# Routing the Gelu experts of a four-stage transformer kernel, and spreading the spline weights' preparation

## What is computed

```python
# layer 0: neighbourhood attention; layer 2: window attention with a bias and a mask
# layer 1: Gelu experts, 2 shared and 8 routed, each token takes its best 2
hs = gelu(einsum('td,nfd->ntf', t, sw1) + sb1); shared = einsum('ntf,ndf->td', hs, sw2) + sb2.sum(0)
probs = softmax(t @ gate_w.T + gate_b); top_v, top_i = top_k(probs, 2)
routed = sum over the two chosen e of top_v * (gelu(t @ rw1[e].T + rb1[e]) @ rw2[e].T + rb2[e])
# layer 3: spline experts, 8, each token takes its best 2
spline = einsum('nic,oic->no', b_splines(x), spline_w * scaler[..., None])
```

## Time and profile before

| | us |
|---|---|
| median of 3 runs | 1057.26 |
| lowest, highest | 1048.71, 1076.12 |
| span of the profiled execution | 1046.9 |
| busy: PE, DVE, ACT, POOL | 937.1, 663.3, 632.8, 377.1 |

### The profile page before, as it was taken

How to read it: one execution, slowest core, us unless ns; L and a number is a source line. 1 busy time by engine, 2 the same in 40 slices (tenths; PEclk the granted TensorE clock), 3 DMA queues, 4 the chain that set the end, 5 groups by cost and what they waited for, 6 DMA issues and landing times. The chain is left out here.

```text
span 1046.9 us, 23408 instructions
## 1 busy us (share of the span) xinstructions
PE 937.1 (90%) x8217; PEld 864.7 (83%) x8217; DVE 663.3 (63%) x1339; ACT 632.8 (60%) x1665; POOL 377.1 (36%) x298
## 2 busy tenths in 40 slices
PE   4776888999998886888979999999999999999993
PEld 3655777889987775766449999999999999999992
DVE  4766675452566534555854877877777777777762
ACT  5993433334442434996135788777777777777751
POOL 1225693882956911331011123223333323332111
PEclk9995898999999987675979999999999999999997
DMA  2002736458447330001134554531535442530000
GB/s 74 3 2 67 301 157 275 183 200 366 192 173 332 136 136 13 3 2 45 44 111 179 190 200 139 196 116 34 192 100 193 134 161 95 193 100 13 7 7 8
DMA packets 25100, 132.67 MB, mean 127 GB/s; under 512 B 3258, under 2 KB 14788, under 8 KB 17876
## 3 DMA queue, kind: packets, MB, share of 16 engines
q0 software_dynamic: 11152, 65.54, 17.5%
q1 hardware_dynamic: 13892, 66.39, 17.3%
HBM read 98.83 MB, written 33.10 MB: 126 GB/s over the span
## 5 line engine op out<-in xcount | busy, mean ns | idle before, releaser
L1242 PE MATMUL kan_ps_h<-kan_xf,kan_w 128*128 128x128 f32 x2496 | 304.4, 275 | 2.0 <-DMA kan_w<-w_dram 2.0
L1242 PEld LDWEIGHTS kan_ps_h<-kan_xf,kan_w 128*128 128x128 f32 x2496 | 291.2, 192 | 2.8 <-DMA kan_w<-w_dram 2.8
L675 ACT ACTIVATE f_hid<-f_ps_up,f_wt 128x512 f32<-128x512 f32 x160 | 108.4, 688 | 154.6 <-PE f_ps_up L624 154.4
L1256 PE MATMUL kan_ps_y<-kan_w,kan_hf 128*128 128x128 f32 x1248 | 154.0, 277 | 8.3 <-DVE kan_hf L1394 8.3
L635 PEld LDWEIGHTS f_ps_dn<-f_wt,f_hid 128*128 128x128 f32 x1280 | 149.7, 194 | 6.9 <-issue 3.1
L1256 PEld LDWEIGHTS kan_ps_y<-kan_w,kan_hf 128*128 128x128 f32 x1248 | 147.2, 194 | 8.8 <-issue 8.8
L635 PE MATMUL f_ps_dn<-f_wt,f_hid 128*128 128x128 f32 x1280 | 150.2, 277 | 3.4 <-DVE x_sb L745 3.4
L624 PE MATMUL f_ps_up<-f_n_part,f_w_part 128*128 128x512 f32 x480 | 127.3, 419 | 23.5 <-DVE f_w_part L704 17.4
L1465 POOL DMA_INDIRECT out<-kan_y_sb,kan_slots_y x39 | 63.8, 1636 | 234.5 <-ACT kan_y_sb L1340 234.5
L745 DVE SCALAR_TENSOR_TENSOR x_sb<-f_ps_dn,f_mix_now,x_sb 128x128 f32<-128x128 f32 x160 | 44.6, 343 | 137.6 <-PE f_ps_dn L635 137.4
L624 PEld LDWEIGHTS f_ps_up<-f_n_part,f_w_part 128*128 128x128 f32 x480 | 94.1, 202 | 43.7 <-DVE f_w_part L704 14.8
(11 more groups left out here) (197 smaller groups left out, 1572.7 us busy)
## 6 DMA issues: line engine op xcount, KB each, us to landing
kan_w<-w_dram SPq DMA_DIRECT2D x16, 2304.0 KB, 9.0
sw_raw<-in_experts POOLq DMA_DIRECT2D x8, 3456.0 KB, 15.4
w_dram<-sw_raw POOLq DMA_DIRECT2D x8, 2304.0 KB, 7.3
kan_w<-w_dram SPq DMA_DIRECT2D x16, 1152.0 KB, 5.2
w_dram<-sw_raw POOLq DMA_DIRECT2D x8, 1152.0 KB, 10.1
f_wt<-in_experts SPq DMA_DIRECT2D x10, 514.0 KB, 4.5
sw_scal<-in_scalers POOLq DMA_DIRECT2D x8, 384.0 KB, 16.4
x_sb<-in_x SPq DMA_DIRECT2D x4, 256.0 KB, 3.9
```

Source lines behind the costliest of these rows:

```text
L675: eng.activation(hid[s % 2][:, c, :], ps_up[c][:, :], ACT.Gelu, bias=wt[a][:, 2 * FF0 + c:2 * FF0 + c + 1]).then_inc(acted.sem, 1)
L1242: mm = eng.matmul(ps_h[n % 2][:, m, :], w12[n % 2][:, at:at + P], rhs, start=(c == 0), stop=(c == BASES))
L1256: mm = eng.matmul(ps_y[n % 2][:, :], lhs, w3[n % 2][:, i * P:(i + 1) * P], start=(i == 0), stop=(i == CH1 * FEAT - 1))
```

## The change

1. The Gelu layer runs only the two shared experts over all tiles (8 steps, with two `ps_up` buffers). For the eight routed ones VectorE forms the list of slots beside these steps, as the routing stage does. Then 39 tiles follow: GpSimd gathers 128 token rows from a DRAM copy of the normalised tokens, PE turns them, multiplies up and down in f32, VectorE scales, GpSimd scatters the rows to a DRAM array with two rows per token. SP loads the tile's expert (514 KB and a bias row), four buffers deep. At the end SP loads the two rows per token back and VectorE adds them.
2. The spline weights are prepared in 18 pieces of 128x512 per expert (`SplineWeights.piece`). Experts 0 to 2 are done by GpSimd in attention 0, three pieces a turn from turn 2; 3 and 4 by VectorE among the 39 tiles, two pieces a tile in tiles 0 to 8 and 30 to 38; 5 to 7 by GpSimd in attention 1 from turn 3. SP issues all their loads and stores. The window biases are added by VectorE in tiles 13 to 27.

```diff
@@ attention, GpSimd's loop
                     normalise(i - 5)
+                    beside(eng, i)
@@ build, attention 0 (attention 1: experts 5 to 7, i - 3 and i - 2)
+                def load0(eng):
...
+                    prep.load(eng, 0)
+                    prep.load(eng, 1)
+                    prep.store(eng, 0)
+                    prep.load(eng, 2, 0)
+                    prep.store(eng, 1)
+                    prep.store(eng, 2)
+                    for e in range(3):
+                        eng.wait_ge(prep.stored[e], 32)
...
+                def beside0(eng, i):
+                    for j in range(3 * (i - 2), 3 * (i - 1)):
+                        if 0 <= j < 3 * prep.PIECES:
+                            prep.piece(eng, j // prep.PIECES, j % prep.PIECES)
@@ SplineWeights
+    def store(self, eng, e):
+        eng.wait_ge(self.done[e], self.PIECES)
...
+    def piece(self, eng, e, j):
...
+        if j == 0:
+            eng.wait_ge(self.loaded[e], 32)
+        if j < BASES:
+            eng.tensor_tensor(first[:, j, :], first[:, j, :], scal[:, 0:SCAL12], ALU.mult).then_inc(self.done[e], 1)
...
@@ gelu_experts, SP
+                for n in range(SLOT_TILES):
+                    if n >= W_BUFFERS:
+                        eng.wait_ge(r_down, n - W_BUFFERS + 1)
+                    lot = eng.value_load(lots[0:1, n:n + 1], min_val=SHARED, max_val=SHARED + EXPERTS - 1)
+                    eng.dma_start(wt[n % W_BUFFERS][:, :], d["experts0"][bass.ds(lot, 1), :, :])\
+                       .then_inc(in_w[n % W_BUFFERS], 16)
...
+                    if n == 14:
+                        prep.store(eng, 3)
+                    if n == 22:
+                        prep.load(eng, 4, 3)
@@ gelu_experts, PE: turn_x waits for the gathered rows, tile_down for ScalarE's Gelu
+                turn_x(0)
+                turn_x(1)
+                tile_up(0)
+                for n in range(SLOT_TILES):
+                    turn_x(n + 2)
+                    tile_up(n + 1)
+                    tile_down(n)
@@ gelu_experts, GpSimd (X_BUFFERS is 4)
+                for n in range(X_BUFFERS):
+                    gather_x(n)
+                eng.wait_ge(slots_ok, 1)
+                for n in range(SLOT_TILES):
+                    scatter_y(n)
+                    gather_x(n + X_BUFFERS)
```

More of the change, by code:

```diff
@@ L487, in rank_experts, with gelu_experts @@
     first = earlier.rearrange("p (a b) -> p a b", b=EXPERTS).unsqueeze(1).to_broadcast(shape)
[L488 to L496, removed]
+    eng.tensor_tensor(above, other, own, ALU.is_gt)
+    chain.after(eng.tensor_tensor(level, other, own, ALU.is_equal))
+    chain.after(eng.tensor_tensor(level, level, first, ALU.mult))
+    chain.after(eng.tensor_tensor(above, above, level, ALU.add))
+    chain.after(eng.tensor_reduce(rank[:, :, :], above, X, ALU.add))
+def gelu_experts(nc, sems, clear_after, software, x_sb, consts, d, prep, make_bias, to_clear, stats, normed_dram, y_dram,
+                 pos1, mask1, s_tab):
     ident = consts[:, C_ID:C_ID + P]
+    ones = consts[:, C_ONES:C_ONES + P]
     with ExitStack() as own:
@@ new lines, in gelu_experts @@
+        picked = sb("picked", wide)
+        base = sb("base", wide)
+        total = sb("total", wide)
+        upto = [sb(f"upto{i}", wide) for i in range(2)]
+        many = sb("many", [P, EXPERTS, TILES])
+        tiles_of = sb("tiles_of", [P, EXPERTS])
+        before = sb("before", [P, EXPERTS, EXPERTS])
+        start = sb("start", [P, EXPERTS])
+        begun = sb("begun", [P, SLOT_TILES, EXPERTS])
+        owner = sb("owner", [P, SLOT_TILES])
+        lots = sb("lots", [P, SLOT_TILES], U32)
@@ L597, in _ @@
                 mm.then_inc(gated, 1)
[L598 to L615, removed]
@@ new lines, in _ @@
+                eng.wait_ge(counted, 1)
+                chain.after(eng.tensor_copy(total[:, :, :], ps_total))
+                chain.after(eng.tensor_copy(upto[0][:, :, :], total[:, :, :]))
+                a, step = 0, 1
+                while step < TILES:
+                    new, old = upto[1 - a], upto[a]
+                    eng.tensor_copy(new[:, 0:step, :], old[:, 0:step, :])
+                    chain.after(eng.tensor_tensor(new[:, step:, :], old[:, step:, :], old[:, 0:TILES - step, :],
+                                                  ALU.add))
+                    a, step = 1 - a, 2 * step
@@ new lines, in _ @@
+                chain.after(eng.tensor_reduce(start[:, :], before[:, :, :], X, ALU.add))
+                chain.after(eng.tensor_scalar(start[:, :], start[:, :], float(P), None, ALU.mult))
+                shape = [P, SLOT_TILES, EXPERTS]
+                chain.after(eng.tensor_tensor(begun[:, :, :], start[:, :].unsqueeze(1).to_broadcast(shape),
+                                              starts.unsqueeze(2).to_broadcast(shape), ALU.is_le))
+                chain.after(eng.tensor_reduce(owner[:, :], begun[:, :, :], X, ALU.add))
```

739 lines of the change are left out of this document (481 added, 258 removed).

## The result

The changed kernel takes 1091.8 us (median; 1086.91 to 1100.78). The kernel before has a median of 1066.69 in the same comparison, but two of its four runs (1076 and 1085 us) were slow ones, and the ratio, 1.0406 with a 95% interval of [1.0286, 1.0525], is taken from fast runs alone. The change is slower, as forecast; the forecast of 1078 was 14 us short. The profiled execution has a span of 1085.1 us, 38.2 longer than before's 1046.9 (forecast: 1073).

The account below looks back on a forecast made before the run. PE was taken to bound the Gelu layer, with GpSimd becoming the bound of attention 0. Attention 0 +27, attention 1 +33 and Gelu layer -34 gave +26 us on a span of 1046.9: 1073, plus 5 for 1078 us, range 1025 to 1122.

Parts of the forecast that it names:

- Attention 0, +27 forecast: Attention 0: first piece at about 20 us, GpSimd's 54 pieces, then the last store; stage ends near 116.5, +27 us.
- the loss of 0.3 at each normalisation: Attentions: GpSimd and VectorE's normalisation take turns, GpSimd losing some 0.3 us a time, 4.8 us for the stage.
- Attention 1, +33 forecast: Attention 1: the same 54 pieces, multiplications and additions between load and last store; 120 us against 87.5, +33.
- the store of expert 4 takes 6 us of the stage before the load: Attention 1: expert 4's store reaches 6 us into the stage, weights land at 7, the first expert's load at 17.
- Gelu layer, -34 forecast: Gelu layer: first y at 89 us, tiles 167, store and load 7, tail 17; 280 against 313.9, -34.
- The mechanism of the tile loop: Gelu layer's 39 tiles: gather n+4 stands behind scatter n on GpSimd; 8.8 us for two turns, 4.4 a tile.
- the way from y to GpSimd's scatter: Tile loop: y on VectorE, 0.28 us for a 128x128 and two semaphores, 0.6 us of the 8.8 for two tiles.
- need less: Tile loop: the tile weights, 514 KB a tile in four buffers, have three turns and need less than the chain.
- The spline store and load: Tile loop: expert 3's store and expert 4's load share the tile weights' queue and delay some tiles, +7 us.
- The loop at its floor: Rival, 0.20: tile loop at 3.25 us a tile, not 4.4; sum -22 us, 1030; decides from 3.7 a tile down.
- The blocked normalisation: Rival, 0.17: VectorE's normalisation enters only when GpSimd stops; +36 us in attention 0, +4 in attention 1, 1118 us.
- The half clock: Rival, 0.18: PE at half clock through the tile loop, with the longer scatter; 5.15 us a tile, +29, 1107 us.

Follow-up runs that it names:

- the run of the tiles alone: Changed kernel without VectorE's 36 pieces in the tile loop, expert 3's weights stored as loaded for experts 3 and 4 before that loop: 1071.91 us.
- the exchange of two lines: Changed kernel with GpSimd's gather for tile n+4 issued ahead of the scatter of tile n: 1030.46 us, 0.9794 of the kernel before.
- the run that loads them once: Changed kernel without loads of tile weights from the fifth tile on, later tiles using the experts of the first four: 1052.16 us.
- another order of GpSimd's work: Changed kernel with GpSimd in turn n gathering for tile n+4 and scattering tile n-2: 1018.02 us.
- the last version: Changed kernel, scatter two tiles behind, 36 pieces per attention, others in the Gelu layer, expert 4's store and expert 5's load in nine transfers each: 967.67 us.

## Why the prediction was right, and where it was off

- **Sign and shape.** Two attentions that cost what the Gelu layer can't pay back: this is what happened, and each part of it was shown by an experiment of its own. That the total came no further off than 12 us is partly luck, since misses cancelled: the attentions came out 11 us cheaper than forecast, the Gelu layer 18 dearer and the routing 5.
- **Attention 0, +27 forecast, +22.8 measured.** The start (20; 18.9), the piece (1.2; 9.84 / 8 = 1.23) and the store (11; 12.0) hold. The step that failed is the loss of 0.3 at each normalisation, 4.8 us in all: GpSimd's three pieces and a multiplication take 4.68 in every turn, met by a normalisation or not. The 0.3 came from comparing two different instructions: 1.29 is a bias addition, 1.04 the multiplication in attention. VectorE alone loses: 0.34 us where GpSimd stands still, up to 1.44 here. The kernel before had the same meeting in most turns of attention 0, and GpSimd's 1.04 was already its price beside VectorE (timeline before):

```profile
29.38 1.13 DVE L423 TENSOR_SCALAR a_xn<-x_sb,a_ln_moments,a_ln_rstd 128x128 f32<-128x128 f32 x1
29.39 1.04 POOL L395 TENSOR_TENSOR a_weights<-a_probs,a_total 128x512 f32<-128x512 f32 x1 [3.21 <-DVE a_total L443]
```

- **Attention 1, +33 forecast, +26.1 measured.** The load was there at 16.2 (17 forecast), the stage's end came 10 us after the last piece (11). The same 4.8 were not there; the multiplication (1.00 from start to start) and the addition (0.41) were a little shorter, too. That the store of expert 4 takes 6 us of the stage before the load was wrong: it is 1.8, by the run of the tiles alone. There the load was ready at 14.4 without that store, and not at some 17 - 6 = 11, so two errors met.
- **Gelu layer, -34 forecast, -16.3 measured.** First y at +89.7 (89) and the tail of 17.3 (17) hold. The mechanism of the tile loop was right: a chain of pairs, closed by GpSimd's order, and shown by the exchange of two lines. Its size was off. The 16 ordinary pairs took 9.79 us in the mean, not 8.8. The term that was mis-sized most is the way from y to GpSimd's scatter (0.6; 1.18, or 11 us over 19 pairs), then the gather (3.4; 3.70, from 2.66 in the short pair to 4.79 in the long one) and the scatter (1.3; 1.49); PE's turn, put midway between its clocks, held as a mean (3.5; 3.41). That the tile weights "need less" was true of their own path and not of what they do to the gathers: 29 us by the run that loads them once. The spline store and load cost 10.8 us more than two ordinary pairs (forecast 7), but not by the queue of the tile weights, as the prediction has it: PE waited for gathered rows, with the tile weights and without.
- **The routing, 0 forecast, +5.2 measured.** Not seen. It is PE's clock: with the same 134 instructions PE was busy 43.58 us at a granted clock of 0.71, where it was 38.05 at 0.81. By the runs it is no fixed cost of the change: the run of the tiles alone had 44.14 us at 0.81, after the same gap of PE. The changed kernel's first products, then those of the tiles alone (timeline of PE), and the routing of the tiles alone (columns as in the earlier trace rows):

```profile
523.50 3.75 PE L1069 MATMUL rt_ps_idle<-consts 128*128 128x512 f32 x4 [9.71 <-PEq L239]
```

```profile
513.77 3.75 PE L1063 MATMUL rt_ps_idle<-consts 128*128 128x512 f32 x4 [9.71 <-PEq L239]
```

```profile
513.65:557.79 44.14, 38.42 (x134) 23.37 (x134) 37.35 (x123) 5.39 (x8) 0.00 (x0) 0.81 0.18 51
```

Over all runs the routing took 43.8 to 44.1 us at 0.81 and 47.2 to 49.2 at 0.71 to 0.75 (53.5, at 0.72, with the store ahead of it). Why the clock differs stays open.

- **The rivals.** The loop at its floor did not come: 5.02 a tile against the 3.7 from which it decides; it took another order of GpSimd's work to get there. The blocked normalisation did not come: it took at most 1.44 us. The Trainium skill (SBUF — State Buffer, section Who interferes with whom) says that the pair of ports the two engines share is held for a whole instruction and the other engine blocks meanwhile; the trace agrees for these rows, since 1.44 is one piece (1.23) and a little more. The half clock came in part: PE's part of a pair was 2.39 in the short one and 4.35 in the long one. The prediction's argument against the floor, that the clock fell whenever PE had gaps, does not fit its own rows: in the first turn of the earlier trace rows PE stood idle for 1.12 of 4.20 us at a granted clock of 1.00.

## What to carry to other kernels

In an in-order queue a prefetch that stands behind a result's store closes a loop: count over how many tiles it closes and divide the chain's length by that, before pricing any single step. Work that is put beside a stage fits only as the sum over its engine's queue, from the first load to the last store: here 36 pieces cost attention 0 nothing and 54 cost 23 us. A bulk transfer costs most where it stands whole in the queue of small loads that others wait for; cut into parts between them it cost a fraction (7 us in place of 23). Look at the row that waits before blaming that queue: in the changed kernel the same store delayed gathers that were issued through another.

## What the runs showed of the hardware

GpSimd was not slowed by VectorE's normalisations in the attentions (4.68 us in every turn of attention 0), but both engines were slowed beside VectorE's list of slots, where the last version's GpSimd prepares expert weights (timeline there, GpSimd and VectorE):

```profile
114.07 7.99 POOL L1086 TENSOR_TENSOR sw_raw<-sw_raw 128x512 f32<-128x512 f32 x4
118.74 2.18 DVE L488 TENSOR_TENSOR f_in_tile<-f_in_tile,consts 128x1024 f32<-128x1024 f32 x1
144.64 26.03 DVE L953 TENSOR_SCALAR f_lane_hot<-consts,f_tile_no 128x128 fp32r<-128x128 f32 x32
162.83 5.20 POOL L1086 TENSOR_TENSOR sw_raw<-sw_raw 128x512 f32<-128x512 f32 x4
```

The same instructions of VectorE in the changed kernel, where GpSimd stands still:

```profile
134.90 1.23 DVE L488 TENSOR_TENSOR f_in_tile<-f_in_tile,consts 128x1024 f32<-128x1024 f32 x1
...
167.45 6.36 DVE L944 TENSOR_SCALAR f_lane_hot<-consts,f_tile_no 128x128 fp32r<-128x128 f32 x32
```

Beside instructions of 1024 wide, of which this one went from 1.23 to 2.18 us, a piece took 2.00 in place of 1.23: both lost. Beside the short comparisons a piece took 1.30, and nearly all the loss was VectorE's: 0.81 us each in place of 0.20.

A plain scatter took GpSimd 0.99 us (1.44 in the long pair), against 1.60 for the one in the earlier trace rows that adds, and 0.30 us in which no wait is seen stand ahead of each indirect DMA that follows another. PE's granted clock in the routing was 0.71 or 0.81 after the same 9.71 us without work; what decides it stays open.
